# Local attention in a merged attention stream: where its mask is added, where its exponentials read, and who copies half of its turned weights

## The reference

```python
x = _layernorm(x + _L0_attn_ref(x, ...)); x = _layernorm(x + _L0_xattn_ref(x, ctx, mask)); x = _layernorm(x + _L0_ffn_ref(x, ...))
x = _layernorm(x + _L1_attn_ref(x, Wq, Wk, Wv, Wo))
x = _layernorm(x + _L1_xattn_ref(x, ctx, Wq, bq, Wkv, bkv, Wp, bp))
x = _layernorm(x + _L1_ffn_ref(x, ...))
```

```python
scores = jnp.einsum('bhnrd,bhncd->bhnrc', qb, kw) * scale
valid = (dist >= 0) & (dist <= window) & (key_global >= 0)
scores = jnp.where(valid[None, None], scores, jnp.finfo(scores.dtype).min)
probs = jax.nn.softmax(scores, axis=-1)
out = jnp.einsum('bhnrc,bhncd->bhnrd', probs, vw)
```

```python
q, k, v = _fq_sym(q, axis=-1), _fq_sym(k, axis=-1), _fq_sym(v, axis=2)
attn = _fq_unsigned(jax.nn.softmax(einsum('bhqd,bhkd->bhqk', q, k)), axis=-1)
out = einsum('bhqk,bhkd->bhqd', attn, v)
```

## Time and profile before

| | |
|---|---|
| time, median of 3 runs | 481.09 us (479.13 to 481.2) |
| profiled execution | 481.17 us, of which 479.2 us is the span from the first to the last instruction |
| busy in the span | PE 375.5 us, DVE 295.9, ACT 210.6, POOL 134.9 |
| granted TensorE clock, mean | 0.888 of full speed |

### The profile page before, as it was taken

One profiled execution on the slowest core, in us unless ns is written; L12 is line 12 of the kernel. 1 busy time (PEld: TensorE's weight loads), 2 busy tenths in 40 slices (PEclk: granted clock), 3 DMA queues, 4 the chain that ended last, 5 costly groups with the idle time before them and its releaser, 6 DMA issues.

```text
span 479.2 us, 6706 instructions
## 1 busy us (share of the span) xinstructions
PE 375.5 (78%) x2300; PEld 223.8 (47%) x2323; DVE 295.9 (62%) x604; ACT 210.6 (44%) x537; POOL 134.9 (28%) x256
## 2 busy tenths in 40 slices
PE   5986978289987989787878756648685698999993
PEld 2544457144443556454545534314343443565572
DVE  4994398959624676675665639878896273122234
ACT  2673221272245635556353537559898512010000
POOL 6248646828570012201414001341212000000002
PEclk9988796879998698887696979898898999999997
DMA  8992110670000000232352095598999502211211
GB/s 242 313 355 27 1 2 1 221 306 1 0 1 0 1 1 1 45 67 44 65 69 46 0 155 78 100 150 164 165 153 166 173 1 99 66 45 44 66 44 44
DMA packets 84896, 42.19 MB, mean 88 GB/s; under 512 B 73536, under 2 KB 80640, under 8 KB 84416
## 3 DMA queue, kind: packets, MB, share of 16 engines
q1 hardware_dynamic: 82560, 41.71, 36.8%
q0 software_dynamic: 2304, 0.07, 1.4%
HBM read 21.58 MB, written 2.88 MB: 51 GB/s over the span
## 4 chain that ended last, share of the span: by engine, by line
PE 48%; DVE 16%; DMA 12%; ACT 8%; issue 7%; POOL 6%; SPq 1%; POOLq 0%; DVEq 0%; ACTq 0%
PE ps L860 25%; PE ps L1256 6%; PE ps L1050 5%; DMA area_a<-area_b 4%; PE ps L1061 4%; ACT area_a L786 3%; ACT area_b L798 3%; POOL deltas L529 2%; DVE small L1520 2%; DMA area_b<-in_idx_row_dram 2%; PE ps L1044 2%; PE ps L1126 2%; PE ps L1155 2%; DVE area_b L1530 1%; DMA area_b<-deltas 1%
## 5 line engine op out<-in xcount | busy, mean ns | idle before, releaser
L1530 DVE CUSTOM_DVE_ANT_0 area_b<-ps,zero,small 128x1024 f32<-128x1024 f32 x64 | 79.9, 1273 | 11.3 <-PE ps L1126 6.1
L798 ACT ACTIVATE area_b<-area_b,small 128x1024 int16<-128x1024 f32 x64 | 73.2, 1145 | 29.9 <-POOL small L613 21.8
L786 ACT ACTIVATE area_a<-ps,small 128x256 f32<-128x256 f32 (+1 forms) x128 | 52.0, 429 | 46.4 <-DVE small L1520 37.9
L1126 PE MATMUL ps<-area_b 128*128 128x512 bf16 x114 | 39.0, 423 | 28.5 <-DVE small L1530 18.9
L860 PE MATMUL ps<-xT_odd,early 128*128 128x512 f32 x128 | 57.3, 594 | 0.0
L1520 DVE TENSOR_REDUCE small<-ps 128x4 f32<-128x1024 f32 (+1 forms) x24 | 29.2, 1217 | 33.7 <-PE ps L1050 33.7
L498 POOL TENSOR_SCALAR var_eps<-meanvar 128x1 f32<-128x1 f32 x24 | 6.7, 281 | 132.1 <-DVE meanvar L1377 132.0
L613 POOL TENSOR_SCALAR small<-small 128x1 f32<-128x1 f32 x64 | 12.4, 194 | 110.6 <-DVE small L1530 110.1
L1654 DVE TENSOR_TENSOR area_b<-ps,area_b 128x512 f32<-128x512 f32 x16 | 11.0, 691 | 51.9 <-ACT area_b L835 51.9
L860 PE MATMUL ps<-area_b,xT_even 128*128 128x512 f32 x64 | 31.5, 638 | 10.3 <-ACT area_b L746 10.3
L835 ACT ACTIVATE area_b<-ps 128x512 f32<-128x512 f32 x16 | 9.5, 596 | 63.4 <-PE ps L860 63.4
(11 more groups left out here) (261 smaller groups left out, 692.7 us busy)
## 6 DMA issues: line engine op xcount, KB each, us to landing
early<-in_w_up_dram SPq DMA_DIRECT2D x1, 4096.0 KB, 16.1
area_b<-gates_out SPq DMA_DIRECT2D x16, 256.0 KB, 3.0
deltas<-area_b SPq DMA_DIRECT2D x1, 2112.0 KB, 17.8
area_b<-deltas SPq DMA_DIRECT2D x2, 1024.0 KB, 5.8
area_a<-in_w_down_dram SPq DMA_DIRECT2D x1, 2048.0 KB, 9.5
early<-in_ctxT_dram SPq DMA_DIRECT2D x1, 1024.0 KB, 15.0
early<-in_ctx_dram SPq DMA_DIRECT2D x1, 1024.0 KB, 13.9
early<-in_w_qkv_dram SPq DMA_DIRECT2D x2, 384.0 KB, 5.9
```

The lines of the kernel that those rows point to most:

```text
L786: a = act.activation(p1[:, n % 2, x * nk * P:(x + 1) * nk * P], slot(k)[:, x * nk * P:(x + 1) * nk * P], ACT.Exp, bias=nmx1[:, n % 2, x:x ...
L798: act.activation(px[:, u % PX, :], sx[:, u % 3, :], ACT.Exp, bias=nbx[:, u:u + 1], accum_out=zx[:, i, h:h + 1]).then_inc(sem("px_ready"), 1)
L1126: mm = pe.matmul(bank(2 * (k % 2) + half), qTx[:, i % 2, h, :], kTx[:, h // 2, half * 512:(half + 1) * 512], start=True, stop=True)
L1530: dve.tensor_tensor_reduce(sx[:, u % 3, :], slot(k), zero[:].broadcast_to([P, B * M]), qsc[:, i, h:h + 1], LOWEST, ALU.add, ALU.max, mxx[: ...
```

## The change

- The mask is no longer added by TensorE. VectorE's maxima become passes of 128 or 256 columns, one for each head, that read scores from PSUM and the mask from SBUF and write their negated sum to `p1`, with the negated maximum beside it. The exponentials then read `p1` in SBUF and write it in place.
- So a local job's slot is free when VectorE has passed over it (`max1_ready`, now two for each job), and all scores run three jobs ahead; `lead` goes. `p1` has three buffers, not two.
- Only the left half of the turned weights is copied by VectorE. The right half is copied by ScalarE, in the step after the job's own, behind that step's exponentials (`evac_right`).
- To make room for the third `p1` buffer there are 6 `pTx` buffers, not 8, and `apply_cross` takes 2 units at a time, not 4, one after the other; both have their outputs in the same 32 partitions.
- The two loads of stage 3 share a semaphore.

```diff
-PT = 8
-BATCH = 4
+PT = 6
+BATCH = 2
...
-        p1 = carve("a", 18 * N, [2, 8 * P])
+        p1 = carve("a", 18 * N, [3, 8 * P])
...
-        def lead(k):
-
-            return 3 if k >= 3 and jobs[k - 2][0] == "X" else 2
...
                         else:
                             quantise(n)
+                    if 1 <= k <= len(jobs) and jobs[k - 1][0] == "L":
+                        evac_right(jobs[k - 1][1])
...
-                act.wait_ge(sem("max1_ready"), n + 1)
-                if n >= 2:
-
-                    act.wait_ge(sem("pT1_ps"), 2 * (n - 1))
...
-                    a = act.activation(p1[:, n % 2, x * nk * P:(x + 1) * nk * P], slot(k)[:, x * nk * P:(x + 1) * nk * P],
-                                       ACT.Exp, bias=nmx1[:, n % 2, x:x + 1], accum_out=z1[:, i, h:h + 1])
+                    if x % (len(heads) // 2) == 0:
+                        act.wait_ge(sem("max1_ready"), 2 * n + 1 + x // (len(heads) // 2))
+                    own = p1[:, n % 3, x * nk * P:(x + 1) * nk * P]
+                    a = act.activation(own, own, ACT.Exp, bias=nmx1[:, n % 3, x:x + 1], scale=-1.0, accum_out=z1[:, i, h:h + 1])
...
+            def evac_right(n):
+
+                if n >= 3:
+
+                    act.wait_ge(sem("o1_ps"), (n - 3) // 2 + 1)
+                act.wait_ge(sem("pT1_ps"), 2 * n + 2)
+                act.activation(pT1[n % 3][:, 4 * P:8 * P], bank(5), ACT.Copy).then_inc(sem("pT1_right"), 1)
...
-                            pe.wait_ge(sem("p1_ready"), 2 * (n + 1))
+                            pe.wait_ge(sem("max1_ready"), 2 * (n + 1))
...
-                    for x in range(2):
-                        pe.matmul(bank(2 * (k % 2) + x), ident_b[:], window[:, nk - 1, :], start=True, stop=False)
...
-                                           start=False, stop=b == nk - 1)
+                                           start=True, stop=True)
...
-                            pe.wait_ge(sem("pT1_ready"), 2 * n + x - 1)
+                            pe.wait_ge(sem("pT1_right" if x else "pT1_left"), n)
...
-                    pe.wait_ge(sem("pT1_ready"), 4 * (m + 1))
+                    pe.wait_ge(sem("pT1_left"), 2 * (m + 1))
+                    pe.wait_ge(sem("pT1_right"), 2 * (m + 1))
...
-                    for early_one, late_one in ((0, 2), (1, 3)):
+                    c, pair = divmod(unit5(units[0])[1] // 2, P // PAIR)
+                    for u in units:
                         for k in range(KT):
-                            for u in (units[early_one], units[late_one]):
-                                h = unit5(u)[1]
-                                c, pair = divmod(h // 2, P // PAIR)
...
-                scores(0)
-                scores(1)
+                for k in range(3):
+                    scores(k)
...
-                    for ahead in (2, 3):
-                        if k + ahead < len(jobs) and lead(k + ahead) == ahead:
-                            scores(k + ahead)
+                    if k + 3 < len(jobs):
+                        scores(k + 3)
...
-                    if n >= 2:
-
-                        dve.wait_ge(sem("p1_ready"), 2 * (n - 1))
-                    dve.tensor_reduce(nmx1[:, n % 2, 0:8 // nk], slot(k).rearrange("p (h k) -> p h k", k=nk * P),
-                                      AX.X, ALU.max, negate=True).then_inc(sem("max1_ready"), 1)
+                    if n >= 3:
+
+                        dve.wait_ge(sem("pT1_ps"), 2 * (n - 2))
+                    for x in range(8 // nk):
+                        own = slice(x * nk * P, (x + 1) * nk * P)
+                        m = dve.tensor_tensor_reduce(p1[:, n % 3, own], slot(k)[:, own], window[:, nk - 1, 0:nk * P], -1.0, -LOWEST,
+                                                     ALU.add, ALU.min, nmx1[:, n % 3, x:x + 1])
+                        if x % (4 // nk) == 4 // nk - 1:
+                            m.then_inc(sem("max1_ready"), 1)
...
-                    for x in range(2):
-                        dve.wait_ge(sem("pT1_ps"), 2 * n + x + 1)
-                        dve.tensor_copy(pT1[n % 3][:, 4 * x * P:4 * (x + 1) * P], bank(4 + x)).then_inc(sem("pT1_ready"), 1)
+                    dve.wait_ge(sem("pT1_ps"), 2 * n + 1)
+                    dve.tensor_copy(pT1[n % 3][:, 0:4 * P], bank(4)).then_inc(sem("pT1_left"), 1)
```

More of the change, by code:

```diff
@@ L213, in build @@
         wide_z = carve("spare", 5 * N + DC * P, [2, D])
-        nmx1, z1, rz1 = tiny([2, 2 * HU]), tiny([TT, H1]), tiny([TT, H1])
+        nmx1, z1, rz1 = tiny([3, 2 * HU]), tiny([TT, H1]), tiny([TT, H1])
         vTx = carve("a", 13 * N, [DC, B * M])
@@ L237, in build @@
         pTx = [carve(where, at, [KT * P], I16)
-               for where, at in (("a", 0), ("a", N), ("a", 22 * N), ("a", 23 * N), ("b", 12 * N), ("b", 13 * N), ("spent", 0))]
+               for where, at in (("a", 0), ("a", N), ("b", 12 * N), ("b", 13 * N), ("spent", 0))]
         pTx.append(sb("pTx_last", [P, KT * P], I16)[:])
@@ L389, in _ @@
             load("ctx", ctx_tok, t["ctx"].rearrange("(k p) d -> p k d", p=P))
-            load("w_router0", w_router0[:], t["w_router0"].rearrange(two, p=P))
-            load("w_ffn0", w_ffn0, t["w_ffn0"].rearrange(two, p=P))
+            load("w_router0", w_router0[:], t["w_router0"].rearrange(two, p=P), of="stage3")
+            load("w_ffn0", w_ffn0, t["w_ffn0"].rearrange(two, p=P), of="stage3")
             load("wq1", wq1, t["wq1"].rearrange(two, p=P), of="stage4")
@@ L978, in stage3 @@
             def stage3():
-                pe.wait_ge(sem("in_w_router0"), 16)
-                pe.wait_ge(sem("in_w_ffn0"), 16)
+                pe.wait_ge(sem("in_stage3"), 2 * 16)
                 pe.wait_ge(sem("nb2_ready"), TT)
@@ L1057, in turn @@
                         if n:
-                            pe.wait_ge(sem("pT1_ready"), 2 * n + x - 1)
+                            pe.wait_ge(sem("pT1_right" if x else "pT1_left"), n)
                         for y in range(4):
-                            mm = pe.transpose(bank(4 + x)[:, y * P:(y + 1) * P], p1[:, n % 2, (4 * x + y) * P:(4 * x + y + 1) * P], ident[:])
+                            mm = pe.transpose(bank(4 + x)[:, y * P:(y + 1) * P], p1[:, n % 3, (4 * x + y) * P:(4 * x + y + 1) * P], ident[:])
                         mm.then_inc(sem("pT1_ps"), 1)
@@ L1149, in apply_cross @@
                         enter()
-                    for early_one, late_one in ((0, 2), (1, 3)):
+                    c, pair = divmod(unit5(units[0])[1] // 2, P // PAIR)
+                    for u in units:
                         for k in range(KT):
-                            for u in (units[early_one], units[late_one]):
-                                h = unit5(u)[1]
-                                c, pair = divmod(h // 2, P // PAIR)
-                                mm = pe.matmul(bank(7)[pair * PAIR:(pair + 1) * PAIR, D + c * P:D + (c + 1) * P], ivh[:, k * HX + h, :],
-                                               pTx[u % PT].bitcast(F16)[:, k * P:(k + 1) * P],
-                                               start=early_one == 0 and k == 0, stop=early_one == 1 and k == KT - 1)
+                            mm = pe.matmul(bank(7)[pair * PAIR:(pair + 1) * PAIR, D + c * P:D + (c + 1) * P],
+                                           ivh[:, k * HX + unit5(u)[1], :], pTx[u % PT].bitcast(F16)[:, k * P:(k + 1) * P],
+                                           start=u == units[0] and k == 0, stop=u == units[-1] and k == KT - 1)
                     mm.then_inc(sem("ox_ps"), 1)
```

4 lines of the change are left out of this document (2 added, 2 removed).

## The result

The changed kernel takes 461.78 us (median of 4 runs, 455.22 to 470.04) beside 481.14 for the kernel before; ratio 0.9515, interval 0.940 to 0.963. Measured again in the second group of experiments: 455.38 us (6 runs, 453.38 to 463.99), ratio 0.9472, interval 0.942 to 0.952. Ratios leave disturbed runs out, so they are not those of the medians. The forecast was 470 us, a ratio of 0.977. The sign and the mechanism were right; the gain, some 25 us by the second ratio (0.0528 x 481.17), is twice the forecast of 11.5.

The account below looks back on a forecast made before the run. Bounds: TensorE in the first window, a chain of waits in the middle, VectorE and ScalarE near full in the cross window. Terms -2.5 - 10 + 1 = -11.5 from 481.17 gave 469.7, said as 470 us; range 455 to 486.

Parts of the forecast that it names:

- VectorE's work: Attention stream: passes take 2.4 or 1.7 us a local job, replacing 1.89; net +1 us over the stream.
- The room: First two windows of the stream: VectorE has 17 and 32 us of room beside its net +1 us.
- the middle's round: Jobs 16 to 41: VectorE needs 8.6 us per five jobs; with waits and tile work 10.6, so 55 us in all.
- The two allowances: Jobs 16 to 41: 5 us added for lower-clock spells, 4 for new waits as the apply comes twice as often.
- The slot: Local jobs' PSUM banks, freed by VectorE's pass instead of the exponentials: loop falls from 4.7 to some 2.8 us.
- First window: First 12 local jobs, TensorE the bound: 6.4 us of masks could go, first cross scores 5 us earlier; net -2.5 us.
- Cross window and apply: Cross jobs alone: serial apply at 0.067 us a matmul adds 17 us, covered by TensorE's room; fewer buffers, net +1 us.
- Rival E: Cross apply: serial matmuls take 0.136 us each, costing +17 instead of +1, 486 us in all; chance 0.05.
- ScalarE: Attention stream: 24 copies, 14.3 us, and exponentials dearer from SBUF by 4 us in all, hidden in its room.
- Rival D: Turned weights' right half: TensorE waits for ScalarE's copy; fully exposed 28 us, 498 us in all; chance 0.10.
- Rival B: Middle window: query DMA, norms and VectorE's 7.58 us stall take over, gain eaten, 479 to 483 us; chance 0.12.
- Rival C: TensorE keeps 2.4 GHz with shorter gaps: -6, -18 and 0 in the three windows, about 457 us; chance 0.15.

Follow-up runs that it names:

- The version with my prices: The changed kernel with one extra VectorE reduction, result unused, ahead of each local job's passes: 464.10 us, ratio 0.9692.
- idle products: 54 matmuls that nothing reads, added on TensorE: 458.73 us in the changed kernel, 485.33 us in the kernel before.
- the later queries: The changed kernel with the transposing DMAs of tile 2's and tile 3's queries put later in SP's queue: 453.73 us, ratio 0.9375.
- `lead` and the later queries: The changed kernel with scores two or three ahead and tile 2's and 3's query DMAs later: 451.12 us; with 54 unread TensorE matmuls too, 450.99 us.

## Why the prediction fell short

**The step that failed: VectorE's work.** "Net per job +0.5 (128, 8 jobs) and -0.2 (256, 16 jobs): 4 - 3 = +1 us over the stream, beside 17 and 32 us of VectorE's room." Both halves were wrong. The price: 1.7 and 1.4 us a job, under my lower bounds of 2.1 and 1.6, so the net is 8 x (1.7 - 1.89) + 16 x (1.4 - 1.89) = -9.4 us. The bound had been drawn from the slope between the durations of two long passes; passes in a row overlap. The trace of the kernel before had a row that shows it, of the very copy whose duration I took, four of 0.28 us in 0.88, so 0.20 apart:

```profile
143.94 0.88 DVE L1510 COPY area_a<-ps 128x128 f32<-128x128 f32 x4 [2.82 <-PE ps L860]
```

The room: it hides nothing. With 10.4 us put back the time rose by 10.6 +- 3.5, with 16 us of copies by 13.6 +- 3.3. The version with my prices stands at 0.9692, 466.3 us, where the forecast was 469.7: the term is most of the shortfall (10.6 of 13.9 us). The room was the larger half. The measured price would have moved my sum only through the middle's round, 26 / 5 x 2 x 0.3 = 3.1 us; in the first window the sum had no term for VectorE at all. By stretches, in the profile of that version (the fastest of its six runs): A is 4.8 us shorter than before, where I had the first cross scores 5 earlier, and B 13.9, where I had 10, less the 2.5 that come back behind these scores.

**Why there is no room.** VectorE is busy 49 of 65 to 70 us in B, TensorE 51 to 57, and yet the passes, the copies and the masks cost nearly their length: the mask's 12.7 us on TensorE cost 10.6 +- 3.5. Some 12 us of idle products on the same engine cost 0.1 +- 4.4. The two kernels add 48 and 54 matmuls of the same shape, at like clocks (0.91 to 0.93 and 0.92 to 0.94 over their runs), and are 10.5 +- 4.5 us apart, so the place counts and not the amount. The masks stand after the wait for the slot and ahead of the scores, so the slot's loop (scores, pass, scores of the job after next) is longer by each; the idle products stand mostly ahead of the turns, outside it. That this is the reason is argued, not shown: no run moves one and the same work in and out of the loop. I counted the loop for the slot and then judged the passes by VectorE's idle share.

**The two allowances.** I added "5 us for spells at the lower clock" and "4 for new waits" to the middle. The waits did not come: over the stream the applies wait 1.3 us for VectorE's reads of bank 7, in the changed kernel as in the kernel before. Whether the clock allowance was wrong stays open: B takes 65.0 us at 0.95 and 70.3 at 0.86 in two profiles of the same code, while the kernel before with idle products has a higher clock in B and no shorter B.

**The slot.** Right: it was the chain, 22.2 +- 3.4 us of it by itself. The parts do not add up: slot 22.2, copy 13.6, mask 10.6, against 25 in all. Each was undone alone, and I take it that its chain then is the longest; no two were undone together.

**First window.** By its own sign, first cross scores 3 to 6 us earlier, this step was wrong; its mechanism held in part. Projection and first cross scores, beside the earlier trace rows:

```profile
178.50 1.13 PE L864 MATMUL ps<-wqx,spare 128*128 128x256 f32 x4
...
191.38 0.63 PE L1128 MATMUL ps<-area_b 128*128 128x512 bf16 x1 [5.49 <-DMA area_b<-xT_even]
```

The cross scores came 8.6 us earlier, not 5, and TensorE stood there longer, 5.49 us instead of 2.86, as I had said. But "TensorE is the bound" was read from 44.67 busy us at a clock of 0.86; the masks put back cost nothing there at 0.99. And the term can't be told to 2 us: with the same code up to the first cross scores, A took 44.4, 45.5, 51.3 and 54.0 us at 0.87, 0.84, 0.73 and 0.68.

**Cross window and apply.** Right. One apply of 16 matmuls at the upper clock, from the timeline, beside the earlier trace rows:

```profile
223.16 1.07 PE L1155 MATMUL ps<-area_b 128*32 128x128 f16 x16
```

That is 0.067 us each, the value taken: the whole share of the partner is lost. The Trainium skill, TensorEngine Tiling (Array Packing), Key Properties, says that different tiles can run loads and matmuls in parallel, and this trace agrees: with a partner in other partitions 0.033 us each, without one 0.067. The cover held: C changed by 0 and 0.8 us, and alternating again gained nothing. Rival E is out.

**ScalarE.** The prices were right: 14 us of new copies (24 x 0.59) and dearer exponentials. That they are hidden fits the gain, but no run takes them away. The exponentials are 0.387 and 0.497 us, against 0.36 and 0.47 in the earlier trace rows. Two in a row, from the timeline:

```profile
152.21 0.39 ACT L783 ACTIVATE area_a<-area_a,small 128x128 f32<-128x128 f32 x1
...
152.60 0.39 ACT L783 ACTIVATE area_a<-area_a,small 128x128 f32<-128x128 f32 x1
```

They start 0.39 us apart, in the earlier trace rows 0.34. The Trainium skill, VectorE: DVE Perf Modes, section on the TRN2 errata, gives ScalarE 52 cycles more of fixed cost from SBUF than from PSUM, an estimated 43 ns; by that rule the 0.05 us of these rows is what was to be expected, and the trace agrees.

Rival D is out: TensorE waits 0.4 us in all for the copy on ScalarE, and its move there gains 13.6 us. Rival B is out by size, though one of its chains is real: the stall in SP's queue, 4.7 +- 3.7 us. Rival C has the nearest time, 457. Its condition, a higher clock, came in B (0.76 before, 0.86 and 0.95 after) and not in A (0.87; 0.87 and 0.84). Idle products, which raise the clock and are work as well, gave nothing in either kernel; how much of B's gain the clock holds stays open.

**Left out of the sum.** The rest, untouched, took 102.7 us before and 107.7 and 104.4 after. It is scatter and not the change: 102.7 with the later queries, 105.9 in the kernel before with idle products. In single profiles it hides part of the gain.

## What to carry to other kernels

Price a row of short instructions by the distance of their starts in a row of like ones, as the trace of the kernel before had it; where a trace has none, let the lower bound go below the slope of durations. Don't take an engine's idle share for room in the loop that hands a buffer to and fro: here 12.7 us ahead of the scores cost 10.6 +- 3.5, some 12 us mostly ahead of the turns 0.1 +- 4.4. And look through a queue for an entry that waits for something later than its neighbours do; moving two transfers was worth 4.7 +- 3.7 us here.

## What the runs showed of the hardware

The same instructions took 44.4 to 54.0 us in A, by the level of TensorE's clock. In the longest case the fall follows an idle stretch of 1.86 us. From the timeline, local scores of the kernel with the later queries:

```profile
147.37 1.14 PE L1051 MATMUL ps<-area_a,w_keys 32*128 32x512 f32 x8 [0.32 <-DVE area_a L1509]
150.37 3.76 PE L1051 MATMUL ps<-area_a,w_keys 32*128 32x512 f32 x8 [1.86 <-DVE small L1521]
...
155.96 2.08 PE L1051 MATMUL ps<-area_a,w_keys 32*128 32x256 f32 x8
```

In the changed kernel's first profile, after the same 1.86 us of idling, the next four took 1.13 us, the upper level of 2.4 GHz, and the fall came only with the transposes of 152.34 (eight take 1.09 us at the upper level, 1.97 at the lower):

```profile
149.60 1.13 PE L1051 MATMUL ps<-area_a,w_keys 32*128 32x512 f32 x4 [1.86 <-DVE small L1521]
...
152.34 1.79 PE L1062 MATMUL ps<-ident,area_a 128*128 128x128 f32 x8
```

Idle products brought A to 42.9 us at 1.00 in one profile and, with `lead` and the later queries, to 49.3 at 0.90 in the other. C took 94.0 us at 0.89 in the first and 88.5 at 0.98 in the second, so the slow C does not follow from the products; why the clock differs between executions of the same code was not tested.
